# Eight PSUM banks shared out anew in the first layer of a four-layer attention kernel

## The chip, the cores and the metric

One core of one Trainium2 chip (trn2). The metric is the device time of one execution in microseconds; lower is better. All data are float32.

## The reference, cut to what matters

Four layers run one after another on x (16 x 112 x 256) with a context (16 x 375 x 256). The change is in the first layer. For each batch entry it computes, in essence:

```
xn  = layernorm(x) * gamma
q, k, v, ff = split(xn @ w_fused)          # 16 heads of 64, one shared k and v head, 2 x 1024 for the feed-forward
o   = softmax(causal(rope(q) * 64**-0.5 @ rope(k).T)) @ v
y   = x + o @ w_attn_out + (silu(gate) * value) @ w_ff_out
qc  = (layernorm(y) * gamma) @ w_q ;  kc, vc = split((layernorm(context) * gamma_ctx) @ w_kv)
oc  = softmax(qc * 64**-0.5 @ kc.T) @ vc   # 112 queries against 375 keys, 16 heads
z   = y + oc @ w_out + (silu(gate2) * value2) @ w_ff2
```

The first attention is called own, the second cross.

## The kernel before, in words

Every engine runs a program of its own, written out by hand; semaphores alone join them. A layer is one block, and the next layer starts when all engines have ended it. Layer 0 (`layer0`, L551) takes two batch entries at a time, in `TURNS` = 8 turns; seven of them are the body of a loop on each engine, the last stands behind it.

PSUM has eight banks of 128 x 512 float32. `Ring` (L73) shares some of them out to a list of jobs: job k uses bank k modulo the number of banks, and before TensorE writes it, it waits (`Ring.free`, L93) until the job that used that bank last has been read (`emptied`). Layer 0 has three rings, made at L634 and L635:

- the scores ring `S`: 40 items a turn, 8 of the own phase (four heads in one bank) and 32 of the cross phase (one head each);
- the ring `TR` of transposed probabilities, two banks;
- the product ring `P`: everything else, 69 jobs a turn in the order in which TensorE issues them.

The jobs of `P` in the own phase are f0 to f7 (a gate tile and a value tile of the feed-forward, eight matmul instructions, `project` L499), cT00 to cT11 (transposed context, L735, which write at L740), and sO00 to sO13 (outputs of four heads each). In order: f0 f1 cT00 f2 cT01 sO00 f3 cT10 sO01 f4 cT11 sO02 f5 sO03 f6 sO10 f7 sO11 OT00 OT01 sO12 sO13. Then y0 OT10 OT11 y1 ck0 cv0 ck1 yT cv1, cq0 to cq3, cf0 to cf7 (the last two in the cross phase), cO00 to cO13 with cOT00, cOT01 and xT between them, and at the end of the turn k z0 cOT10 cOT11 v0 v1 q0a q0b z1 q1a ... q3b for the coming turn.

`Attention.tensor` (L290) issues, in step s: scores(s), the transposes of item s-2 (`turns`, L306, write at L313), the values of item s-3 (`values`, L316), and then the side work: f(s), and in steps 1 to 4 one cT. ScalarE (`scalar`, L353) does in step s: the tanh of f(s-1) (`gate`, L862, write at L869), the exponentials of item s (L366, L373), the copy pT of item s-2 (L377), and the copy of the cT. VectorE (`vector`, L381) does in step s: the maxima of item s (L392, which reads the score bank and empties it, and L394; in the cross phase L401, and there ScalarE's L373 empties the bank), then hidden(s-1) (`hidden`, L992: L998 and L1000, the last one empties f(s-1)), then in the cross phase the copy pT (L405), and the outputs of item s-3 (L416, L419). The order within an engine is fixed, so what stands behind a waiting instruction waits too.

The other lines named below: L161 is the matmul of every `project`, L301 and L303 the scores, L331 and L335 the values, L721 and L724 the two halves of an output y or z (`outputs`, L716), L732 the transposed outputs OT, read by ScalarE at L873, L893 ScalarE's copy of v, L1004 VectorE's addition that reads y or z, L1025 VectorE's reading of q, L690 GpSimd's addition of q.

```
def earlier(k, depth, count):
    if k >= depth:
        return k - depth, True
    return max(m for m in range(count) if m % depth == k % depth), False
...
self.lagged(phases, [(0, scores), (LAG_T, turns), (LAG_V, values)], between)
...
self.lagged(phases, [(0, maxima), (0, amid), (LAG_T, turned), (LAG_V, outputs)], between, amid)
```

Of the kernel before, what the change touches and what calls it, by code (L numbers as in the profile page):

```python
# [22 lines left out]
class Signal:  # L23
# [3 lines left out]
    def __init__(self, ctx, nc, name, per_turn):  # L27
        self.sem, self.per_turn = ctx.enter_context(nc.semaphore(name)), per_turn

    def prime(self, eng):  # L30
        if self.per_turn:
            eng.sem_inc(self.sem, self.per_turn)
# [132 lines left out]
def wide(ap, axis, n):  # L165

    ap = ap.unsqueeze(axis)
    shape = list(ap.shape)
    shape[axis] = n
    return ap.to_broadcast(shape)  # L170
# [47 lines left out]
class Attention:  # L218
    def __init__(self, ctx, nc, layer, phases, scored, turned, P):
        self.phases, self.P = phases, P  # L220
        self.owner = [(ph, k) for ph in phases for k in range(ph.items)]
# [29 lines left out]
    def pT_free(self, turn, m):  # L251
# [3 lines left out]
        if ph.closes(k):  # L255
            ring = ph.ring or self.P
            s, n = ring.full, ring.index[ph.job(k)]
# [32 lines left out]
    def tensor(self, pe, i, phases, ident, between=None):  # L290
# [25 lines left out]
        def values(ph, k):  # L316
            m = ph.first + k
            j, r = ph.at(k)
            job, P = ph.job(k), ph.ring or self.P
            bank, w = P.bank(job), ph.dh + 1  # L320
            if ph.val_ready:
                for sem, count in counts(i, *ph.val_ready(k)):
                    pe.wait_ge(sem, count)
            if ph.grouped or r % G == 0:
                for sem, count in P.free(i, job, TR.got(m)):
                    pe.wait_ge(sem, count)
# [224 lines left out]
def layer0(nc, c, x_in, context, x_out, w, prefetch):  # L551
# [5 lines left out]
    ctx = ExitStack()  # L557
    with ctx:
# [19 lines left out]
        banks = [ctx.enter_context(nc.psum_tensor(f"l0_bank{b}", [128, 512], F32)) for b in range(8)]  # L578
# [26 lines left out]
        def cross_values_ready(k):  # L605
            return [P.got(f"cv{k // H}")] if k % H == 0 else []

        own = Phase("s", True, H, DH, lambda j, h: qT[:, h // 2, j * T:(j + 1) * T], lambda j, h: kz[:, j, h % 2, :],
                    lambda j, h, t: v[:, j, :], own_ready, bias=lambda r: wide(c.causal[:T, :], 1, G), val_ready=own_values_ready)
        cross = Phase("c", False, H, DH, lambda j, h: qT[:, h // 2, j * T:(j + 1) * T], lambda j, h: ckz[:, j, h % 2, :],  # L610
                      lambda j, h, t: cv[:, j, t, :], cross_ready, val_ready=cross_values_ready)
# [11 lines left out]
        def own_job(s):  # L623
            return [(own.job(s - LAG_V), "dve")] if s >= LAG_V else []
# [4 lines left out]
        jobs = [job for s in range(own.items + LAG_V) for job in own_job(s) + beside_own.get(s, [])] + chain \  # L629
# [1 line left out]
        names = [job for job, _ in jobs]  # L631
        before_x = names[:names.index("xT")]
        after_x = names[names.index("xT") + 1:names.index("k")]
        P = Ring(ctx, nc, "l0_product", banks[4:8], jobs)  # L634
        A = Attention(ctx, nc, "l0", [own, cross], banks[0:2], banks[2:4], P)  # L635

        x_come, c_come, z_sent = signal("x_come", 16), signal("context_come", 16 * PAIR), signal("z_sent", 16)
        NORMS = ("y", "x", "c")
# [76 lines left out]
        def _(pe):  # L715
# [11 lines left out]
            def output_turned(i, j, half, name, done):  # L727
                for sem, count in P.free(i, name, P.got(done)):
                    pe.wait_ge(sem, count)
                for n in range(4):  # L730
                    t = 4 * half + n
                    last = pe.transpose(P.bank(name)[:, n * T:(n + 1) * T], A.O[:, j, t * 128:(t + 1) * 128], c.ident[:T, :T])  # L732
                last.then_inc(P.full.sem, 1)
# [35 lines left out]
            def own_side(i, s):  # L769
                if s < 8:  # L770
                    project(pe, P, i, f"f{s}", [columns(V["wff"], s), columns(V["wff"], 8 + s)], xT)
                if 1 <= s <= 4:
                    context_turned(i, (s - 1) // KT, (s - 1) % KT)
                if s == 8:
                    for half in range(2):
                        output_turned(i, 0, half, f"OT0{half}", own.job(own.groups - 1))

            def between_phases(i):
                pe.wait_ge(weights.sems["out"], weights.count("out"))
                outputs(i, "y0", 0, V["wao"], V["wfo"], "f7", "OT01")  # L780
                for half in range(2):
                    output_turned(i, 1, half, f"OT1{half}", own.job(own.items - 1))
                outputs(i, "y1", 1, V["wao"], V["wfo"], "f7", "OT11")
                pe.wait_ge(weights.sems["cross"], weights.count("cross"))
                context_keys(i, 0)
                context_values(i, 0)
                context_keys(i, 1)
                turn_tokens(pe, c, P, i, "yT", xhat, normed.this(NORMS.index("y")))
                context_values(i, 1)
                for t in range(HT // 2):  # L790
                    project(pe, P, i, f"cq{t}", [columns(V["wq2"], 2 * t), columns(V["wq2"], 2 * t + 1)], xT, P.got("yT"))
                for f in range(6):
                    gate_and_value(i, f)
# [4 lines left out]
            def cross_side(i, s, coming):  # L798
                if s < 2:
                    gate_and_value(i, 6 + s)  # L800
                elif s in (22, 26):
                    output_turned(i, 0, (s - 22) // 4, f"cOT0{(s - 22) // 4}", cross.job(H - 1))
                elif s == 30:
                    if coming:
                        turn_tokens(pe, c, P, i, "xT", xhat, normed.this(NORMS.index("x")))
                    else:
                        P.pass_over(pe, "pe", i, ["xT"])

            def turn_ending(i, coming):
                if coming:  # L810
                    keys(i)
                else:
                    P.pass_over(pe, "pe", i, ["k"])
                pe.wait_ge(weights.sems["cross_out"], weights.count("cross_out"))
                outputs(i, "z0", 0, V["wo2"], V["wf2"], "cf7", "cOT01")
                for half in range(2):
                    output_turned(i, 1, half, f"cOT1{half}", cross.job(cross.items - 1))
                if coming:
                    values(i)
                    queries(i, 0)  # L820
                else:
                    P.pass_over(pe, "pe", i, ["v0", "v1", "q0a", "q0b"])
                outputs(i, "z1", 1, V["wo2"], V["wf2"], "cf7", "cOT11")
                if coming:
                    for t in (1, 2, 3):
                        queries(i, t)

            def turn(i, coming):
                A.tensor(pe, i, [own], c.ident, lambda s: own_side(i, s))
                between_phases(i)  # L830
                A.tensor(pe, i, [cross], c.ident, lambda s: cross_side(i, s, coming))
                turn_ending(i, coming)

            prime(pe, "pe", [A.S, A.TR], [A.values])
            pe.wait_ge(zeroed, 4)
# [18 lines left out]
        def _(act):  # L854
# [40 lines left out]
            def gate_before(i, s):  # L895
                if 1 <= s <= 8:
                    gate(i, s - 1)

            def own_side(i, s):
                if 1 <= s <= 4:  # L900
                    context_turned(i, (s - 1) // KT, (s - 1) % KT)
                if s == 8:
                    for half in range(2):
                        output_turned(i, 0, half, f"OT0{half}")

            def between_phases(i):
                for half in range(2):
                    output_turned(i, 1, half, f"OT1{half}")
                context_keys(i, 0)
                context_values(i, 0)  # L910
                context_keys(i, 1)
                tokens_turned(i, "yT", c.column["L0_gamma_ca"])
                context_values(i, 1)
                for t in range(HT // 2):
                    name = f"cq{t}"
                    act.wait_ge(P.full.sem, P.count_full(i, name))
                    act.activation(qT[:, 2 * t:2 * t + 2, :].rearrange("p a b -> p (a b)"), P.bank(name)[:, 0:2 * TP],
                                                 ACT.Copy, scale=DH ** -0.5).then_inc(P.emptier(name).sem, 1)
                for f in range(6):
                    gate(i, 8 + f)  # L920
# [12 lines left out]
            def turn_ending(i, coming):  # L933
                for half in range(2):
                    output_turned(i, 1, half, f"cOT1{half}")
                if coming:
                    values(i)
                else:
                    P.pass_over(act, "act", i, ["v0", "v1"])

            def turn(i, coming):
                A.scalar(act, i, [own], lambda s: own_side(i, s), lambda s: gate_before(i, s))
                between_phases(i)
                A.scalar(act, i, [cross], lambda s: cross_side(i, s, coming))
                turn_ending(i, coming)
# [2013 lines left out]
```

## Time and profile before

| | |
|---|---|
| median of 3 runs | 4230.74 us (4230.36 to 4244.27) |
| the profiled execution | 4239.7 us, span 4238.0 us |
| TensorE matmuls (PE) | 3909.1 us busy, 92% of the span |
| VectorE (DVE) / ScalarE (ACT) | 1881.8 us, 44% / 1614.5 us, 38% |
| granted TensorE clock, mean | 0.959 of full speed |
| layer 0 in the trace | 0 to about 1250 us |

All rows are of the one profiled execution. PE is a matmul on TensorE, PEld a weight load that runs beside matmuls, DVE is VectorE, ACT ScalarE, POOL GpSimd. Times are microseconds from the start of the span. The ends of matmuls are modelled, so the start of a weight load is the best mark of when TensorE goes on to a new group. A clock of 1.00 is 2.4 GHz, 0.50 is 1.2 GHz.

### The profile page before, as it was taken

Reading aid. Unit: us, or ns where it says so; the run is one execution under the profiler, and the core shown is the slowest. Engines: PE = TensorE matmul, PEld = TensorE weight load, DVE = VectorE, ACT = ScalarE, POOL = GpSimd, SP = SyncE. Lnnn points to the kernel's source line nnn. Section 1 sums busy time; section 2 is a strip of 40 time slices with the busy share of each in tenths; the row PEclk is TensorE's granted clock in tenths of the full one; section 3 lists DMA queues with packets and bytes.
Section 4 is the critical chain, followed back from the end, with each engine's and each line's share of the span. In section 5 each row is a group of like instructions: output and inputs, shape, how many; then the busy total and the mean of one; then the engine's idle time right before and its main releaser. Section 6 shows DMA issues by size and latency. Waiting matters only on the chain. (4 is left out here: it accounts for less than half of the span.)

```text
span 4238.0 us, 68913 instructions
## 1 busy us (share of the span) xinstructions
PE 3909.1 (92%) x23128; PEld 3193.6 (75%) x23128; DVE 1881.8 (44%) x5419; ACT 1614.5 (38%) x3709; POOL 320.5 (8%) x379
## 2 busy tenths in 40 slices
PE   7999999999978999999996999999999997888888
PEld 6888888888867778888774777777777775666666
DVE  3554544545434544555542323323323323546544
ACT  2232333323323433334332454454454443333333
POOL 1000000000001111001100000000000001111110
PEclk9999999999997999999998999999999998899998
DMA  4000000000002000000002000000000000000000
GB/s 167 4 10 13 10 4 13 11 3 13 3 24 94 13 8 12 12 5 12 10 3 75 7 13 7 7 13 7 7 13 7 7 7 21 11 16 16 15 14 5
DMA packets 64014, 75.10 MB, mean 18 GB/s; under 512 B 8336, under 2 KB 61168, under 8 KB 62704
## 3 DMA queue, kind: packets, MB, share of 16 engines
q1 hardware_dynamic: 63728, 71.42, 5.4%
q8 instruction: 163, 2.67, 0.3%
q14 instruction: 123, 1.01, 0.1%
HBM read 64.01 MB, written 7.40 MB: 17 GB/s over the span
## 5 line engine op out<-in xcount | busy, mean ns | idle before, releaser
L313 PEld LDWEIGHTS l_bank<-identity,l_p 112*125 112x125 f32 (+1 forms) x3456 | 516.6, 178 | 244.3 <-issue 18.5
L335 PE MATMUL l_bank<-l_cv,l_pT 125*112 125x65 f32 (+2 forms) x5376 | 640.7, 253 | 54.4 <-ACT l_pT L377 45.4
L161 PE MATMUL l_bank<-l_xT,weights_of_layers_and 128*128 128x224 f32 x3072 | 665.3, 371 | 27.2 <-ACT l_xT L2643 8.5
L335 PEld LDWEIGHTS l_bank<-l_cv,l_pT 125*112 125x112 f32 x5376 | 601.6, 178 | 69.0 <-ACT l_pT L377 32.3
L161 PEld LDWEIGHTS l_bank<-l_xT,weights_of_layers_and 128*128 128x128 f32 x3072 | 595.5, 199 | 55.3 <-ACT l_xT L2643 10.1
L313 PE MATMUL l_bank<-identity,l_p 112*125 112x112 f32 (+1 forms) x3456 | 545.3, 270 | 8.8 <-ACT l_p L366 7.7
L373 ACT ACTIVATE l_p<-l_bank,l_nm 112x375 f32<-112x375 f32 x512 | 293.3, 573 | 487.1 <-DVE l_nm L401 486.6
L303 PE MATMUL l_bank<-l_ckT,l_qz 128*112 128x375 f32 x1024 | 424.3, 498 | 7.2 <-DVE l_qz L1518 7.2
L370 ACT ACTIVATE l_p<-l_p,l_nm 112x375 f32<-112x375 f32 x384 | 233.2, 607 | 470.6 <-DVE l_nm L398 469.2
L366 ACT ACTIVATE l_p<-l_p,l_nm 112x112 f32<-112x112 f32 x768 | 234.8, 376 | 431.8 <-DVE l_nm L394 431.5
L401 DVE TENSOR_REDUCE l_nm<-l_bank 112x1 f32<-112x375 f32 x512 | 279.8, 546 | 204.6 <-PE l_bank L303 201.3
L377 ACT ACTIVATE l_pT<-l_bank 125x336 f32<-125x336 f32 (+1 forms) x576 | 266.4, 464 | 42.8 <-PE l_bank L313 42.8
L161 PE MATMUL l_bank<-l_cT,weights_of_layers_and 128*128 128x375 f32 x704 | 262.8, 500 | 19.9 <-ACT l_cT L2047 17.8
L398 DVE CUSTOM_DVE_ANT_0 l_p<-l_bank,weights_of_layers_and 112x375 f32<-112x375 f32 x256 | 139.1, 543 | 280.4 <-issue 279.5
L405 DVE COPY l_pT<-l_bank 125x336 f32<-125x336 f32 x512 | 254.7, 497 | 14.7 <-PE l_bank L313 13.2
L161 PE MATMUL l_bank<-weights_of_layers_and,l_cT 128*125 128x512 f32 (+2 forms) x768 | 249.2, 462 | 0.0
L460 POOL TENSOR_TENSOR l_ve<-l_mv,eps 112x2 f32<-112x2 f32 (+1 forms) x89 | 17.3, 195 | 2944.4 <-DVE l_mv L454 2944.4
L303 PE MATMUL l_bank<-l_ckz,l_qT 128*112 128x375 f32 x512 | 211.6, 495 | 0.1
L331 PE MATMUL l_bank<-l_v,l_pT 112*112 112x65 f32 (+1 forms) x1536 | 187.1, 262 | 23.2 <-ACT l_pT L377 21.0
L331 PEld LDWEIGHTS l_bank<-l_v,l_pT 112*112 112x112 f32 x1536 | 179.2, 189 | 33.7 <-issue 32.3
L161 PE MATMUL l_bank<-weights_of_layers_and,l_OT 128*112 128x256 f32 x704 | 174.7, 401 | 26.3 <-ACT l_OT L2654 15.9
L303 PEld LDWEIGHTS l_bank<-l_ckT,l_qz 128*112 128x112 f32 x1024 | 152.1, 177 | 58.0 <-issue 28.9
(244 smaller groups left out, 4859.6 us busy)
## 6 DMA issues: line engine op xcount, KB each, us to landing
l_cx<-in_ctx SPq DMA_DIRECT2D x64, 375.0 KB
x_after_layer<-l_z SPq DMA_DIRECT2D x24, 224.0 KB, 2.4
l_x<-x_after_layer SPq DMA_DIRECT2D x24, 224.0 KB, 2.7
weights_of_layers_and<-in_L_xattn_w_fused SPq DMA_DIRECT2D x1, 2048.0 KB, 9.8
weights_of_layers_and<-in_L_xattn_w_ff SPq DMA_DIRECT2D x1, 2048.0 KB, 12.0
weights_of_layers_and<-in_L_xattn_lin_W SPq DMA_DIRECT2D x2, 1024.0 KB, 11.6
weights_of_layers_and<-in_L_xattn_sa_wkv SPq DMA_DIRECT2D x1, 2048.0 KB, 16.3
weights_of_layers_and<-in_L_xattn_ca_wkv SPq DMA_DIRECT2D x1, 2048.0 KB, 21.2
```

What stands on the lines that cost most here:

```text
L161: last = pe.matmul(out, left, right, start=(k == 0), stop=(k == len(pairs) - 1))
L303: last = pe.matmul(bank[:T, 0:S2], ph.q(j, r), ph.k(j, r), start=True, stop=True)
L313: last = pe.transpose(bank[:ph.keys, g * T:(g + 1) * T], p[:, m % PD, g * ph.keys:(g + 1) * ph.keys], ident[:T, :T])
L331: last = pe.matmul(bank[:T, g * w:(g + 1) * w], pT[:T, m % PD, g * T:(g + 1) * T], ph.val(j, r * G + g, 0), start=True, stop=True)
L335: last = pe.matmul(bank[:T, g * w:(g + 1) * w], pT[:ph.keys, m % PD, t * T:(t + 1) * T], ph.val(j, r, t), start=(t == 0), stop=(t == ph.ti ...
L366: last = act.activation(own, own, ACT.Exp, bias=nm[:, c:c + 1])
L370: act.activation(own, own, ACT.Exp, bias=nm[:, ph.col0 + k:ph.col0 + k + 1], scale=-1.0).then_inc(self.probs.sem, 1)
L373: act.activation(p[:, m % PD, 0:S2], S.bank(m)[:T, 0:S2], ACT.Exp, bias=nm[:, ph.col0 + k:ph.col0 + k + 1]).then_inc(S.emptier(m).sem, 1)
L377: self.turned(act, i, ph, k, lambda out, src: act.activation(out, src, ACT.Copy))
L398: dve.tensor_tensor_reduce(p[:, m % PD, 0:S2], S.bank(m)[:T, 0:S2], ph.bias(r), -1.0, 3.0e38, ALU.add, ALU.min, nm[:, ph.col0 + k:ph.col0 ...
L401: dve.tensor_reduce(nm[:, ph.col0 + k:ph.col0 + k + 1], S.bank(m)[:T, 0:S2], AX.X, ALU.max, negate=True).then_inc(self.neg_max.sem, 1)
L405: self.turned(dve, i, ph, k, lambda out, src: dve.tensor_copy(out, src))
```

## The change

The first layer's banks are shared out anew: scores three banks for two, products three for four; the ring of transposed probabilities keeps two, but other ones. Nothing else differs; the waits follow from the number of banks.

```
-        P = Ring(ctx, nc, "l0_product", banks[4:8], jobs)
-        A = Attention(ctx, nc, "l0", [own, cross], banks[0:2], banks[2:4], P)
+        P = Ring(ctx, nc, "l0_product", banks[5:8], jobs)
+        A = Attention(ctx, nc, "l0", [own, cross], banks[0:3], banks[3:5], P)
```

## Rows read from the trace of the kernel before

**Rows 1.** Busy time by stretch, layer 0: stretch, length, busy per engine, clock, DMA.

```profile
0.00:1250.00 1250.00, 1200.76 (x7706) 1065.30 (x7707) 618.26 (x1545) 393.22 (x933) 66.91 (x96) 1.00 0.07 21
```

**Rows 2.** Waits of PE, 47.7 to 1240 us: total, times, longest.

```profile
PE l_bank L313 <- ACT l_p L366: 4.5, 5, 0.9
...
PE l_bank L301 <- DVE l_p L392: 3.4, 5, 1.0
...
PE l_bank L331 <- ACT l_pT L377: 1.8, 5, 0.4
```

**Rows 3.** Busy time by stretch, steady cross phase of turn 1.

```profile
306.00:316.00 10.00, 10.00 (x72) 8.17 (x71) 6.33 (x15) 4.22 (x8) 0.00 (x0) 1.00 0.01 2
```

**Rows 4.** Timeline, turn 0, step 4: start, duration, engine, line; [idle before <-releaser].

```profile
59.77 0.87 PEld L301 LDWEIGHTS l_bank<-l_kz,l_qT 128*112 128x112 f32 x8
...
60.86 0.62 DVE L392 TENSOR_TENSOR l_p<-l_bank,causal 112x448 f32<-112x448 f32 x1 [1.31 <-PE l_bank L301]
...
61.74 1.44 PEld L161 LDWEIGHTS l_bank<-l_xT,weights_of_layers_and 128*128 128x128 f32 x8
...
62.47 0.39 DVE L1000 SCALAR_TENSOR_TENSOR l_hid<-l_u,l_bank 128x224 f32<-128x224 f32 x1
```

**Rows 5.** Timeline, turn 1, steps 2 and 3.

```profile
203.51 0.62 DVE L392 TENSOR_TENSOR l_p<-l_bank,causal 112x448 f32<-112x448 f32 x1 [5.00 <-issue]
...
204.26 1.03 PE L301 MATMUL l_bank<-l_kz,l_qT 128*112 128x112 f32 x8 [0.97 <-DVE l_p L392]
...
204.82 1.22 ACT L366 ACTIVATE l_p<-l_p,l_nm 112x112 f32<-112x112 f32 x4 [25.78 <-DVE l_nm L394]
...
206.19 0.56 PE L313 MATMUL l_bank<-identity,l_p 112*112 112x112 f32 x4 [0.89 <-ACT l_p L366]
...
206.50 1.44 PEld L161 LDWEIGHTS l_bank<-l_xT,weights_of_layers_and 128*128 128x128 f32 x8
...
206.74 0.39 DVE L1000 SCALAR_TENSOR_TENSOR l_hid<-l_u,l_bank 128x224 f32<-128x224 f32 x1
...
207.93 0.44 PEld L740 LDWEIGHTS l_bank<-identity,l_cx 125*128 125x128 f32 x3
...
208.64 0.39 DVE L1000 SCALAR_TENSOR_TENSOR l_hid<-l_u,l_bank 128x224 f32<-128x224 f32 x1
...
210.15 0.97 PE L331 MATMUL l_bank<-l_v,l_pT 112*112 112x65 f32 x8 [0.37 <-ACT l_pT L377]
```

**Rows 6.** Timeline, turn 0, steps 2 and 3.

```profile
55.51 0.44 PEld L740 LDWEIGHTS l_bank<-identity,l_cx 125*128 125x128 f32 x3
...
55.68 0.39 DVE L1000 SCALAR_TENSOR_TENSOR l_hid<-l_u,l_bank 128x224 f32<-128x224 f32 x1
...
57.93 1.44 PEld L161 LDWEIGHTS l_bank<-l_xT,weights_of_layers_and 128*128 128x128 f32 x8
...
58.61 0.39 DVE L1000 SCALAR_TENSOR_TENSOR l_hid<-l_u,l_bank 128x224 f32<-128x224 f32 x1
```

**Rows 7.** Timeline, ending of turn 1.

```profile
330.26 0.42 DVE L1004 TENSOR_TENSOR l_z<-l_bank,l_y 112x256 f32<-112x256 f32 x1 [5.40 <-PE l_bank L724]
...
330.65 0.98 ACT L873 ACTIVATE l_OT<-l_bank 128x448 f32<-128x448 f32 x2 [11.40 <-PE l_bank L732]
330.74 0.86 PEld L161 LDWEIGHTS l_bank<-weights_of_layers_and,l_xT 128*112 128x112 f32 x8
...
331.52 1.63 PEld L161 LDWEIGHTS l_bank<-l_xT,weights_of_layers_and 128*128 128x128 f32 x9
```

**Rows 8.** Timeline, turn 1, between the phases.

```profile
238.63 0.42 DVE L1004 TENSOR_TENSOR l_y<-l_bank,l_x 112x256 f32<-112x256 f32 x1 [6.31 <-PE l_bank L724]
...
239.10 3.30 PEld L721 LDWEIGHTS l_bank<-weights_of_layers_and,l_hid 128*112 128x112 f32 x16
```

**Rows 9.** Turn 5: timeline around a fall of the clock, and one stretch.

```profile
811.03 1.08 PE L301 MATMUL l_bank<-l_kz,l_qT 128*112 128x112 f32 x8 [1.86 <-POOL l_qT L690]
811.80 2.71 PEld L161 LDWEIGHTS l_bank<-l_xT,weights_of_layers_and 128*128 128x128 f32 x8
...
812.00:813.00 1.00, 1.00 (x4) 0.93 (x4) 0.00 (x0) 0.00 (x0) 0.00 (x0) 0.50 0.02 8
```

## The prediction, made before the change was built or run

> **What bounds the kernel now.** I first read the table of stretches for layer 0, the only code that the change touches [rows 1]: TensorE is busy 1200.76 of 1250 us, at a granted clock of 1.00. So layer 0 is TensorE's own program from end to end, and whatever makes TensorE wait there is added to the time. The layers follow one another behind a barrier, so a microsecond lost in layer 0 is lost at the end.
>
> Next the waits of TensorE in the eight turns of layer 0 [rows 2]. Only a few places wait, and one is a wait for a score bank: L301 for DVE L392, 5 times, 3.4 us in all. The others are for data: the transposes for the exponentials (4.5 us), the values for the copied pT (1.8 us). No wait for a product bank (L161 on a reader) stands among them. The cross phase, with 32 of the 40 score items of a turn, is seen in its steady part: 10.00 us busy of 10.00 [rows 3]. There nothing waits, so a third score bank can gain nothing.
>
> The step that matters is one of the own phase, s = 4 of turn 0 [rows 4]. Read it in order of time: the weight load of scores(4) at 59.77; DVE begins with scores(4) at 60.86 (L392, then L394); TensorE begins f4 at 61.74; DVE ends hidden(3), which empties f3's bank, at 62.47 + 0.39 = 62.86. With four banks f4 waited for sO00 and did not need f3's bank. That is the whole case: f4 begins 1.12 us before the previous f bank is empty.
>
> **The change, part by part.** *Scores, two banks to three.* scores(n) waits for item n-3 instead of n-2. It can only remove the wait at scores(2). In turn 1 [rows 5] DVE starts on scores(0) at 203.51 (behind a gap that the trace calls issue, after the loop's jump), frees the bank at 204.13, scores(2) starts at 204.26; exp(0) runs from 204.82 to 206.04 and the transposes of item 0 start at 206.19, having waited 0.89. The exponential depends on DVE's maxima of item 0, not on scores(2). So scores(2) moves up into the gap, the transposes start at the same 206.19, and the 3.4 us of rows 2 become waiting at L313. I take 0. The bounds are 0 and a gain of 3.4 us.
>
> The Trainium skill (Perfetto Trace Analysis, Matmuls) says that independent matmul groups should rotate through different PSUM banks so that emptying one overlaps the next group. For the scores it would have the 3.4 us saved, and the sum below would be 3.4 lower; for the products it speaks against this change. The rows bear it out only for the products.
>
> *Products, four banks to three.* Job k waits for job k-3. Counting along the job list of layer 0 (f0 f1 cT00 f2 cT01 sO00 f3 cT10 sO01 f4 cT11 sO02 f5 sO03 f6 sO10 f7 ...), the new waits are f2 on f0, cT01 on f1, f3 on f2, f4 on f3, f5 on f4, f6 on sO02, f7 on sO03. A wait on a bank ends about 0.13 us after the reader's record: 204.13 to 204.26 [rows 5].
>
> - f4: 62.86 + 0.13 = 62.99 against 61.74 [rows 4]: 1.25 us. It cannot be caught up, as the chain scores(n), maxima(n), hidden(n-1), f(n) closes on itself: scores(n) stands behind f(n-1) in TensorE's program and hidden(n-1) behind maxima(n) in DVE's. From the weight load of scores to f was 61.74 - 59.77 = 1.97 and becomes 62.99 - 59.77 = 3.22. f5 is the same step once more: 1.25.
> - cT01 in turn 0: hidden(1) ends at 55.68 + 0.39 = 56.07, so 56.20 against 55.51 [rows 6]: 0.69. f2 needs hidden(0), done long before.
> - f3 in turn 0: hidden(2) ends at 59.00, moves with scores(3) to 59.69, so 59.82 against 57.93 [rows 6]: 1.89 in all, 1.20 of it new.
> - Sum of turn 0: 0.69 + 1.20 + 1.25 + 1.25 = 4.39.
> - In the turns behind the loop's jump (five like turn 1), f2 meets hidden(0), which ends 206.74 + 0.39 = 207.13: 207.26 against 206.50 = 0.76; cT01 meets hidden(1), 209.03 + 0.13 = 209.16 against 207.93 = 1.23 in all [rows 5]. Of this some 0.4 to 0.5 is taken back, since the values of item 0 waited 0.37 anyway (the weight load a little longer). Then f3 adds 1.25, f4 and f5 1.25 each: 4.5. I use 4.4 for all eight turns.
> - From f6 on, the bank wanted is one that DVE empties a step earlier: no wait. While TensorE stands, ACT and DVE stand too, as they wait for scores. What is late next is scores(n+1) and through it everything; no later wait of the turn absorbs it, since those in the cross phase follow from TensorE's own order.
>
> So 8 x 4.4 = 35.2 us. *The ending of a turn* [rows 7]: v0 now waits for z0, emptied at 330.68: 330.81 against 330.74, 0.07. v1 waits for cOT10 (first of two copies, 330.65 + 0.49 = 331.14) against 330.74 + 0.07 + 0.39: 0.07. q0a waits for cOT11 (331.63 + 0.13 = 331.76) against 331.52 + 0.14: 0.10. Together 0.24, in 7 turns 1.7. *Between the phases* [rows 8]: y1 waits for y0's addition, 239.05 + 0.13 = 239.18 against 239.10: 0.08, in 8 turns 0.6. Every other job of the chain and of the cross phase finds job k-3 read at least one product earlier; what hides these is a product of TensorE's between them, and without it each would cost about the 0.4 us of a reader. The number of instructions, DMAs and bytes is the same, and SP, POOL and ACT issue what they did.
>
> *The clock.* In one turn TensorE stood for 1.86 us in one piece ahead of scores(0); a microsecond later the granted clock was 0.50 (1.2 GHz), and the eight weight loads of an f took 2.71 us [rows 9] instead of 1.44, so 1.27 more. In turn 1 the waits of 0.97 and 0.89 had scores(2) between them, and the clock stayed. With scores(2) moved ahead, those two waits become one of about 2 us in five turns, followed by the wait at f2. From below this costs 0, from above 5 x 1.27 = 6.4, or more if a part of the turn is hit twice. Nearest is the row of 1.86 us, but other work of the stretch (the wait at cT01) covers some of it: I take 2.5.
>
> **Sum:** 35.2 + 1.7 + 0.6 + 2.5 = 40.0 us. Made against the profiled execution's 4239.7 us (span 4238.0) this gives 4279.7; the median of the three runs, 4230.74, is 9.0 lower, and the forecast for the median is 4270.7, say 4271, or 0.95% more. No change could be told from this within some 0.5%, 21 us.
>
> **Rivals.** *A, not slower.* One mechanism: DVE reads f(n-1) early enough, so that no product waits. For it: no wait for a product bank shows today, and DVE is busy only about half of the time [rows 1]. Against it: in rows 4 hidden(3) stands behind maxima(4) in DVE's program and ends 1.12 us late. It decides from the point where hidden(n-1) ends by 61.6 in step 4. Then only the score bank counts: between 4227.3 (3.4 gained) and 4231. If even the waits of 4.5 and 1.8 fell, 4221. Chance 0.03.
>
> *B, a part only.* The stalls come at f4 and f5, but what is lost at cT01 and f3 is taken back in slack that the records don't show (the starts on TensorE are modelled): 8 x 2.5 = 20, less the 3.4: 4247 to 4251. For it: the later stall is the clearest, and turn 1 already shows such a giving back. Chance 0.07.
>
> *C, the clock follows the stalls.* Stalls of 1.25 us in three successive steps lower the clock there too. Each f then costs 1.27 more, three of them in eight turns 30 us on top: 4301. For it: rows 9. Against it: the two waits of 1.86 us together in turn 1, with only scores(2) between them, did not lower it in five turns out of five, and the new stalls stand farther apart. Chance 0.06.
>
> *D, the scores gain and the products lose as forecast.* 4267. It lies within the forecast.
>
> **Chances.** The forecast, D within it, 0.84; A 0.03; B 0.07; C 0.06. The range 4252 to 4285: below, the sum with f3 to f5 alone at 1.25, 1.25 and 0.4 (8 x 2.9 = 23) and nothing for the clock; above, 4.9 a turn (nothing taken back) with 6.4 for the clock, 2.3 for the ending and the spread of the three runs. C and most of B lie outside. Faster by over 0.5% would need 21 us gained where all removable waits are 9.7 us: 0.01. Within 0.5% is A and B: 0.09. Slower 0.90.
>
> **What would show it.** In the changed profile TensorE's waits should list L161 on DVE's L1000 (f3, f4, f5 in each of eight turns, 1.0 to 1.25 us each) and L740 on L1000 (8 times), some 33 us together; L301 on L392 gone, and L313 on L366 grown to about 2 us a time; the step of s = 4 (from one weight load of scores to the next) some 1.25 us longer; the cross phase's 10.00 of 10.00 kept; ACT and DVE busy as before; a digit below 1.00 in the clock near the starts of some turns. Wrong would be: no wait of L161 on L1000 (then A), waits of it at f4 and f5 only (B), or f groups of 2.7 us and more in steps 3 to 5 (C).

## The result, and the profile after

The changed kernel takes 4276.85 us in the median (4260.65 to 4282.59, 6 runs), the kernel before 4242.98 us beside it (4230.36 to 4244.80, 6 runs). The ratio is 1.0072, with a 95% interval of 1.0055 to 1.0090: slower by 0.72%, some 30.5 us of 4243; the two medians lie 33.9 us apart. The forecast was 40.0 us, or 0.95%. The profiled execution took 4266.35 us.

From the page of the changed kernel (span, and TensorE's share of it):

```profile
span 4264.6 us, 68681 instructions
...
PE 3909.9 (92%) x23128; PEld 3187.7 (75%) x23128; DVE 1882.2 (44%) x5419; ACT 1615.3 (38%) x3709; POOL 319.7 (7%) x379
```

The spans differ by 4264.6 - 4238.0 = 26.6 us. To see where, I take a mark that both programs have: the first group of transposes of layer 1, as the grouped lines with their first and last times give it. First the kernel before, then the changed one:

```profile
L1298 PE MATMUL l_bank<-identity,context_turned_or_hidden x4: 421/421/448, 1276.3 to 1276.9; 128*128 128x128 f32 x4
```

```profile
L1298 PE MATMUL l_bank<-identity,context_turned_or_hidden x4: 421/421/447, 1308.1 to 1308.7; 128*128 128x128 f32 x4
```

Counted from the first scores (47.9 and 47.5 us), layer 0 takes 1228.4 us before and 1260.6 us after: 32.2 us more. (Ahead of the mark TensorE stands once, for 22.6 to 23.9 us, between the two layers: 23.9 before, 23.5 after. The measure has that stand in it.) What follows the mark, whose code is the same in both, takes 2961.7 and 2956.5 us, 5.2 us less. That second number is no effect. Over all the executions profiled below, the same unchanged stretch takes between 2947.5 and 2975.4 us. So **layer 0 by itself is the finer measure**, and the experiments are read by it: by the time from the first scores to this mark, beside the ratio of the medians.

Now the waits of TensorE in layer 0 (47.7 to 1275 us) in the changed kernel: total, times, longest, to be held against [rows 2].

```profile
PE l_bank L161 <- DVE l_hid L1000: 25.3, 29, 1.0
PE l_bank L301 <- POOL l_qT L690: 10.6, 5, 2.4
...
PE l_bank L301 <- issue: 1.8, 1, 1.8
...
PE l_bank L313 <- ACT l_p L366: 0.9, 3, 0.3
PE l_bank L740 <- DVE l_hid L1000: 0.7, 3, 0.3
```

The first line is new and is the price of the change: an f product (L161) waits for the DVE instruction that empties the bank of the f before (L1000). L301 on L392, the wait for a score bank, is gone. The second line and the `issue` line, six waits of up to 2.4 us at scores(0) of the turns behind the loop's jump, are also longer than before. I had not foreseen that, and it comes back below.

The step s = 4 of turn 0 in the changed kernel, against [rows 4]: start, duration, engine, line, and in brackets the idle time with what ended it.

```profile
60.83 0.87 PEld L301 LDWEIGHTS l_bank<-l_kz,l_qT 128*112 128x112 f32 x8
...
61.92 0.62 DVE L392 TENSOR_TENSOR l_p<-l_bank,causal 112x448 f32<-112x448 f32 x1 [2.43 <-PE l_bank L301]
...
63.53 0.39 DVE L1000 SCALAR_TENSOR_TENSOR l_hid<-l_u,l_bank 128x224 f32<-128x224 f32 x1
63.97 1.43 PEld L161 LDWEIGHTS l_bank<-l_xT,weights_of_layers_and 128*128 128x128 f32 x8 [1.09 <-DVE l_hid L1000]
...
65.81 0.87 PEld L301 LDWEIGHTS l_bank<-l_kz,l_qT 128*112 128x112 f32 x8
```

The loop of the prediction can be read here. The scores go first, DVE takes their maxima (61.92) ahead of hidden(3) (63.53 to 63.92), and only then does the weight load of f4 start (63.97). From scores to f it is 63.97 - 60.83 = 3.14 us where it was 1.97. The next scores start at 65.81, so the step takes 4.98 us. The kernel before had its next scores at 63.58, a step of 63.58 - 59.77 = 3.81 us:

```profile
63.58 0.87 PEld L301 LDWEIGHTS l_bank<-l_kz,l_qT 128*112 128x112 f32 x8
```

In the steady cross phase nothing has changed against [rows 3]:

```profile
313.00:323.00 10.00, 10.00 (x75) 8.34 (x74) 6.71 (x16) 4.34 (x8) 0.00 (x0) 1.00 0.01 2
```

### The profile page after: what moved, and what is told of

The parts are those of the page before. It is cut to its first block and busy times, and to the rows that moved or that the text cites. A ratio compares the mean times of both kernels' runs of the same rounds, so it can differ in the third digit from the quotient of the medians.

```text
span 4264.6 us, 68681 instructions
## 1 busy us (share of the span) xinstructions
PE 3909.9 (92%) x23128; PEld 3187.7 (75%) x23128; DVE 1882.2 (44%) x5419; ACT 1615.3 (38%) x3709; POOL 319.7 (7%) x379
## 5 line engine op out<-in xcount | busy, mean ns | idle before, releaser
L161 PE MATMUL l_bank<-l_xT,weights_of_layers_and 128*128 128x224 f32 x3072 | 660.7, 369 | 61.8 <-DVE l_hid L1000 25.3
L313 PEld LDWEIGHTS l_bank<-identity,l_p 112*125 112x125 f32 (+1 forms) x3456 | 517.6, 178 | 242.1 <-issue 15.5
L335 PE MATMUL l_bank<-l_cv,l_pT 125*112 125x65 f32 (+2 forms) x5376 | 641.7, 253 | 54.1 <-ACT l_pT L377 44.9
L161 PEld LDWEIGHTS l_bank<-l_xT,weights_of_layers_and 128*128 128x128 f32 x3072 | 591.0, 198 | 93.2 <-DVE l_hid L1000 29.7
L313 PE MATMUL l_bank<-identity,l_p 112*125 112x112 f32 (+1 forms) x3456 | 545.7, 270 | 5.4 <-ACT l_p L366 4.3
L366 ACT ACTIVATE l_p<-l_p,l_nm 112x112 f32<-112x112 f32 x768 | 234.7, 376 | 434.4 <-DVE l_nm L394 434.4
L161 PE MATMUL l_bank<-l_cT,weights_of_layers_and 128*128 128x375 f32 x704 | 262.8, 500 | 19.9 <-ACT l_cT L2047 17.9
L161 PE MATMUL l_bank<-weights_of_layers_and,l_cT 128*125 128x512 f32 (+2 forms) x768 | 249.2, 462 | 0.0
L331 PE MATMUL l_bank<-l_v,l_pT 112*112 112x65 f32 (+1 forms) x1536 | 183.4, 260 | 20.3 <-ACT l_pT L377 18.0
L161 PE MATMUL l_bank<-weights_of_layers_and,l_OT 128*112 128x256 f32 x704 | 176.5, 404 | 27.1 <-ACT l_OT L2654 16.1
## 6 DMA issues: line engine op xcount, KB each, us to landing
weights_of_layers_and<-in_L_xattn_lin_W SPq DMA_DIRECT2D x2, 1024.0 KB, 10.3
```

The source lines that it names most:

```text
L161: last = pe.matmul(out, left, right, start=(k == 0), stop=(k == len(pairs) - 1))
L313: last = pe.transpose(bank[:ph.keys, g * T:(g + 1) * T], p[:, m % PD, g * ph.keys:(g + 1) * ph.keys], ident[:T, :T])
L331: last = pe.matmul(bank[:T, g * w:(g + 1) * w], pT[:T, m % PD, g * T:(g + 1) * T], ph.val(j, r * G + g, 0), start=True, stop=True)
L335: last = pe.matmul(bank[:T, g * w:(g + 1) * w], pT[:ph.keys, m % PD, t * T:(t + 1) * T], ph.val(j, r, t), start=(t == 0), stop=(t == ph.ti ...
L366: last = act.activation(own, own, ACT.Exp, bias=nm[:, c:c + 1])
```

## The experiments

### Which of the two parts costs: the product banks alone

```diff
-        P = Ring(ctx, nc, "l0_product", banks[4:8], jobs)
+        P = Ring(ctx, nc, "l0_product", banks[4:7], jobs)
         A = Attention(ctx, nc, "l0", [own, cross], banks[0:2], banks[2:4], P)
```

> Scores keep two banks, products get three (one bank of the eight is left unused). Theory P (the product banks alone cost, the third score bank is worth nothing): the first matmul of layer 1 (L1298) starts about 32 us later than in the kernel before, within 1.5 us of where the changed kernel has it (1308.1), TensorE waits for L1000 about 25 us in all, L301 again waits for L392 about 3 us. Rival R1 (the third score bank gave some of it back): layer 0 is 3.4 us or more longer than in the changed kernel. Rival R2 (the loss needs the moved score or turned banks): layer 0 as before, 1276.

Measured: 1.0063 (1.0044 to 1.0083), layer 0 in 1259.4 us. TensorE's waits:

```profile
PE l_bank L161 <- DVE l_hid L1000: 25.4, 30, 1.0
PE l_bank L301 <- POOL l_qT L690: 8.3, 4, 2.2
```

The whole loss is there with two score banks: 1259.4 against 1260.6 us with three (whose profile has one fall of the clock in layer 0, this one none). One thing I had expected did not come. The wait of L301 on L392 does not return with two score banks; it appears nowhere in the list. At scores(2) TensorE now arrives late by itself, so the second bank is free in time.

### The changed kernel once more

> The changed kernel once more, on the same chip as the three others, so that their layer 0 and times can be held against it. Theory P: ratio 1.006 to 1.009, L1298 starts 30 to 34 us later than in the kernel before, eight turns each with three waits of 0.95 us at L161 for L1000.

This is the changed kernel without any edit, measured together with the kernels on both sides of this section. Measured: 1.0084 (1.0065 to 1.0102), median 4277.13 us, layer 0 in 1260.5 us. Against the 1260.6 us of the first profile this shows how well layer 0 repeats, while the rest of the span came out at 2975.1 us where it had been 2956.5, in the same program.

### Another order on DVE: hidden(n-1) ahead of maxima(n)

The prediction says that f(n) is late because hidden(n-1) stands behind maxima(n) in DVE's program. These two kernels turn that order round, the first with the banks of the change, the second with those of before:

```diff
-        self.lagged(phases, [(0, maxima), (0, amid), (LAG_T, turned), (LAG_V, outputs)], between, amid)
+        self.lagged(phases, [(0, amid), (0, maxima), (LAG_T, turned), (LAG_V, outputs)], between, amid)
```

> The changed kernel, but in the own phase VectorE does hidden(s-1) ahead of maxima(s) in place of behind it. Theory P (f(n) waits through scores(n), maxima(n), hidden(n-1)): f(s-1)'s bank is empty while scores(s) is still computed, so TensorE's waits on L1000 at f3, f4 and f5 go; layer 0 is some 25 to 30 us shorter than in the changed kernel, L1298 starts at 1276 to 1283. Rival R3 (three banks are too few whatever the order, each f waits for its bank's reader in any case): the waits stay at 1 us each and L1298 at 1305 or later.

> The kernel before (two, two, four banks) with hidden(s-1) ahead of maxima(s) on VectorE in the own phase. Theory P: no product waits there before, so the order is worth nothing in the steady steps; in the five turns where exp(0) is late nothing moves either; L1298 at 1276 within 3 us, ratio 1.000 within its interval. Rival: the maxima, and with them exponentials and transposes, come later by up to 0.8 us a step, and TensorE waits at L313: up to 8 x 2 us slower.

Measured: 1.0150 (1.0130 to 1.0170) with three product banks, layer 0 in 1286.3 us; 1.0143 (1.0121 to 1.0165) with four, 1290.7 us. My expectation was wrong for both: the turned order is far slower than either kernel, by 57.9 and 62.3 us in layer 0. TensorE's waits of the first:

```profile
PE l_bank L331 <- ACT l_pT L377: 20.3, 24, 1.3
...
PE l_bank L740 <- DVE l_hid L1000: 11.6, 8, 2.2
PE l_bank L161 <- DVE l_hid L1000: 9.9, 23, 0.5
```

And of the second, with four banks, the largest wait and one round of its steps:

```profile
PE l_bank L331 <- ACT l_pT L377: 43.0, 33, 3.8
```

```profile
62.12 1.22 ACT L366 ACTIVATE l_p<-l_p,l_nm 112x112 f32<-112x112 f32 x4 [2.06 <-DVE l_nm L394]
...
63.26 0.52 ACT L377 ACTIVATE l_pT<-l_bank 112x448 f32<-112x448 f32 x1
...
64.14 0.34 ACT L869 ACTIVATE l_th<-l_bank 128x224 f32<-128x224 f32 x1
64.51 0.39 DVE L998 SCALAR_TENSOR_TENSOR l_u<-l_th,l_bank 128x224 f32<-128x224 f32 x1 [1.88 <-ACT l_th L869]
64.94 0.39 DVE L1000 SCALAR_TENSOR_TENSOR l_hid<-l_u,l_bank 128x224 f32<-128x224 f32 x1
65.24 0.62 DVE L392 TENSOR_TENSOR l_p<-l_bank,causal 112x448 f32<-112x448 f32 x1
...
66.55 1.22 ACT L366 ACTIVATE l_p<-l_p,l_nm 112x112 f32<-112x112 f32 x4 [2.06 <-DVE l_nm L394]
```

Follow the arrows. DVE's hidden waits 1.88 us for ACT's tanh (L869). The tanh stands in ACT's program behind the exponentials and the copy of pT, and the exponentials wait 2.06 us for the maxima (L394). The maxima now stand behind hidden. That is a ring of two engines which closes once a step, in 66.55 - 62.12 = 4.43 us, where a step of the kernel before took 3.81. I had counted TensorE and DVE and had left ACT out. The ring is not all of the loss. Turn 0, which no jump precedes, is 27.36 us long from scores(0) to scores(7) in both kernels where it was 22.80, and eight times 4.56 is 36 us. The rest lies in the turns behind the jump, and the clock has a part in it: it fell six times in layer 0 with three banks and seven times with four, against once in the kernel before.

The test therefore does not isolate the order on DVE, since it makes a ring of its own. It does show that the maxima are put first for a reason. In the first list f(n) waits less for hidden when hidden comes first, 9.9 us at 23 places instead of 25.3 at 29, but the cT waits more, 11.6 us instead of 0.7. Together that is 21.5 against 26.0 us, so this test neither confirms nor refutes that the order on DVE makes the wait. What speaks for it are the rows of the step s = 4 above.

### Two other ways to divide the eight banks

```diff
         P = Ring(ctx, nc, "l0_product", banks[4:8], jobs)
-        A = Attention(ctx, nc, "l0", [own, cross], banks[0:2], banks[2:4], P)
+        A = Attention(ctx, nc, "l0", [own, cross], banks[0:3], banks[3:4], P)
```

The second has `banks[3:8]` for the products, `banks[0:2]` for the scores and `banks[2:3]` for the turned exponentials.

> Scores three banks, products four as before, and the transposed probabilities one bank in place of two. To be read against the next run, which has the one bank too. Theory P: no wait for L1000 at all; TensorE waits at L313 in every step for the copy of the one transposed bank, and layer 0 is longer by that alone. The third score bank is worth nothing: layer 0 within 1.5 us of the next run; L301 no longer waits for L392. Rival R1: it is 3.4 us or more shorter than the next run.

> Scores two banks, transposed probabilities one, products five. Theory P: as the run before it within 1.5 us in layer 0, since neither the third score bank nor the fifth product bank is ever waited for; L301 waits for L392 about 3 us in all at the heads of the turns, and the waits at L313 for L366 there are 3 us longer in the other. Rival R1: 3.4 us or more longer than that one.

Measured: 1.0033 (1.0017 to 1.0049), layer 0 in 1243.2 us, for 3 + 1 + 4 banks; 1.0031 (1.0011 to 1.0050), 1241.3 us, for 2 + 1 + 5. The waits that matter here, first of 3 + 1 + 4, then of 2 + 1 + 5:

```profile
PE l_bank L313 <- ACT l_p L366: 10.3, 6, 2.0
```

```profile
PE l_bank L313 <- ACT l_p L366: 5.4, 6, 0.9
PE l_bank L301 <- DVE l_p L392: 4.1, 6, 0.9
```

This is a second test of the score bank. With two, TensorE waits 4.1 us for it and then 5.4 us for the exponentials; with three it waits 10.3 us for the exponentials. The two waits have merged into one (9.5 and 10.3), as the prediction said, and the time is the same within 1.9 us, a little more than the 1.5 that I had allowed. The two kernels differ in a fifth product bank as well. It has nothing to remove, since no L161 waits for L1000 with four. Both kernels pay 13 to 15 us against before for the single bank of the turned exponentials.

### The loop taken away

Here the turns of layer 0 are written out one after another, with the banks of before (e7) and of the change (e8):

```diff
-            with pe.Fori(0, TURNS - 1) as i:
+            for i in range(TURNS - 1):
```

and so on ACT and DVE, with the scratch cells of the waits used again in each turn.

> The kernel before with layer 0's seven loop turns written out on TensorE, ScalarE and VectorE (GpSimd and SyncE keep their loops). Theory P: the gap of 4.8 to 5.0 us of VectorE at the head of a turn belongs to the jump back, so it goes, and with it the waits of L301 on L392 (3.4), of L313 on L366 (4.5), of L301 on issue and L690 (3.9) and of L331 on L377 (1.8): layer 0 13 us shorter, L1298 at about 1263. Then the third score bank has nothing at all to remove. Rival: the instructions must be fetched all the same and the gaps stay or are spread: L1298 at 1276 or later.

> The changed kernel (3, 2, 3 banks) with layer 0's loop turns written out on TensorE, ScalarE and VectorE. From the first scores (L301) to the first matmul of layer 1 the kernel before takes 1228.4 us, the changed one 1260.6, the kernel before unrolled 1207.6. Theory P: no head of a turn is late, so every turn is like turn 0, which lost 3.7 us; with the ends of the turns 8 x 3.9 = 31 us over the kernel before unrolled: 1238.6 within 2. Rival: part of the loss belongs to the heads of turns (the jump, the merged wait): under 1230.

Measured: 0.9974 (0.9958 to 0.9989), median 4231.26 us (10 runs, 4220.06 to 4234.84), layer 0 in 1207.6 us for the banks of before; 1.0043 (1.0024 to 1.0062), 1238.3 us for those of the change. The waits of TensorE in layer 0, before's banks first:

```profile
PE l_bank L335 <- DVE l_pT L405: 3.0, 8, 0.4
PE l_bank L161 <- ACT l_xT L859: 1.7, 8, 0.2
PE l_bank L721 <- DVEq L129: 1.1, 1, 1.1
```

```profile
PE l_bank L161 <- DVE l_hid L1000: 22.9, 24, 1.0
...
PE l_bank L740 <- DVE l_hid L1000: 1.4, 8, 0.2
```

Without the jump neither kernel waits at the head of a turn, the clock falls in neither inside layer 0, and the change still costs 1238.3 - 1207.6 = 30.7 us; 1238.3 lies within the 1238.6 +- 2 that I had given. So the loss lies in the steady steps, not in the heads. The counts are the predicted ones to the unit: 24 waits of L161 (f3, f4, f5 in eight turns) and 8 of L740 (cT01 in eight turns). The list has 22.9 + 1.4 = 24.3 us. A recorded wait is shorter than what the step loses, 22.9 / 24 = 0.95 against about 1.15 us (below), and 24 x 0.2 = 4.8 us closes most of the gap to 30.7. The ending of a turn (below) has most of what is left.

The kernel before without its loop is the fastest of all that ran. Layer 0 is 20.8 us shorter, where I had expected 13, and 1.3 us of that lie in TensorE's stand ahead of the mark. In the whole only a part of it arrives: the ratio of 0.9974 is some 11 us, and in e8 too the whole is 18 us slower than the kernel before where layer 0 is only 9.9 us longer. What follows the mark took 2972.7 and 2975.4 us in these two profiles, against 2961.7. So the layers behind run some 8 to 10 us longer when layer 0 is written out; the cause stays open.

### Fewer jobs in the steps of the own phase

The stall needs three jobs in a step: one sO, one f and one cT go through a ring of three banks. Here the four cT jobs leave the steps 1 to 4 and go into the chain between the phases, with the same instructions in all. The first kernel has the banks of the change (e9), the second those of before (e10):

```diff
-        for n, name in enumerate(("cT00", "cT01", "cT10", "cT11")):
-            beside_own[n + 1].append((name, "act"))
...
-        chain = [("y0", "dve"), ("OT10", "act"), ("OT11", "act"), ("y1", "dve"), ("ck0", "act"),
+        chain = [("cT00", "act"), ("cT01", "act"), ("y0", "dve"), ("OT10", "act"), ("OT11", "act"), ("y1", "dve"), ("cT10", "act"), ("cT11", "act"), ("ck0", "act"),
```

> The changed kernel (3, 2, 3 banks) with the four cT jobs taken out of steps 1 to 4 of the own phase and put beside y0 and y1, so that two product jobs are issued a step in place of three, and f(n) waits for sO(n-4) in place of f(n-1). Theory P (the wait comes from three jobs a step in three banks): the 25 us of waits on L1000 go; some 0.2 to 0.5 us a turn are new at y0 and ck0; layer 0 within 5 us of the kernel before, L1298 at 1274 to 1281. Rival R3 (three product banks are too few in any order): L1298 at 1300 or later.

> The kernel before (2, 2, 4 banks) with the four cT jobs beside y0 and y1, the control of the run e9. e9 took 1236.8 us from the first scores to layer 1. Theory P: once the third job of a step is gone, three product banks cost almost nothing against four: this run takes 1232 to 1236 (the fall of the clock in two heads of e9, some 3 us, and its wait at the jump not counted). Rival R3: 1228 or less, so that three banks cost 8 us or more even then.

Measured: 1.0023 (1.0007 to 1.0039), layer 0 in 1236.8 us with three product banks; 1.0010 (0.9998 to 1.0022), 1231.1 us with four. TensorE's waits with three:

```profile
PE l_bank L301 <- POOL l_qT L688: 10.5, 5, 2.2
...
PE l_bank L331 <- ACT l_pT L377: 3.5, 7, 0.8
```

L161 on L1000 is gone entirely, and of the 32.2 us that three banks cost, at most 1236.8 - 1231.1 = 5.7 are left. Of these, two falls of the clock in the profile with three, against none in the one with four, are worth about 2 x 1.3 us. So three product banks are enough where a step has two jobs, and one too few where it has three. The kernel with four banks came out at 1231.1 us, just below the 1232 to 1236 that I had given, and not at the 1228 or less of the rival; the difference from before's 1228.4 is 2.7 us, a little more than the repeats show, and is not resolved.

### The head of the turns

In the changed kernel the wait at scores(0) had grown in six turns: from 0.25, 0.73, 0.32, 0.52, 1.86 and 0.22 us (3.9 together) to 1.85, 2.00, 2.28, 2.35, 1.92 and 2.03 (12.4). Turn 1 of the changed kernel, against [rows 5]:

```profile
195.92 2.84 DVE L981 TENSOR_SCALAR l_cx<-l_cx,l_mv,l_rstd 125x256 f32<-125x256 f32 x6
198.67 0.61 DVE L1025 SCALAR_TENSOR_TENSOR l_qT<-l_bank,l_cos 128x448 f32<-128x448 f32 x1
...
203.24 1.03 PE L301 MATMUL l_bank<-l_kz,l_qT 128*112 128x112 f32 x8 [1.85 <-issue]
...
206.96 0.62 DVE L392 TENSOR_TENSOR l_p<-l_bank,causal 112x448 f32<-112x448 f32 x1 [4.90 <-PE l_bank L301]
```

My reading was this. With three banks, the last query product of a turn, q3b, needs the bank of q2a, whose reader stands in DVE's program behind the 2.84 us of the normalisation (L981). The wait moves to the head, but DVE does not begin the new turn before 4.9 us have passed anyway. So I put the normalisation earlier, ahead of z1, in the changed kernel (e11) and in the kernel before (e12):

```diff
+                if coming:
+                    center(i, "c", context_rows, context_rows)
                 add(i, "z1", 1, z, y)
...
-                    center(i, "c", context_rows, context_rows)
```

> The changed kernel with VectorE's normalisation of the context (L981, 2.8 us) ahead of its addition of z1 in place of behind queries 1, so that q2a is read as soon as it is full. In the changed kernel TensorE stands 1.8 to 2.4 us at scores(0) of six turns (before: 0.2 to 0.7 in five, 1.9 in one). Theory J: q3b now waits for q2a, whose reader is late behind the normalisation; that holds TensorE's sequencer back from its jump, and the fetch behind the jump is no longer covered. Then these waits fall to under 1 us. As VectorE's own gap of 4.8 us sets the head of the turn in any case, the time from first scores to layer 1 stays at 1260.6 less at most 2. Rival J2: the 8.5 us of waits were lost time, and 1252 comes out. Rival J3: the waits have another cause and stay.

> The kernel before with the same move of the normalisation. q3b waits for q1b there, read long before, so theory J expects no change: 1228.4 within 1.5 us from first scores to layer 1, waits at scores(0) of 0.2 to 0.7, and a ratio of 1.000 within its interval.

Measured: 1.0085 (1.0055 to 1.0115), layer 0 in 1260.7 us; and 0.9999 (0.9986 to 1.0012), 1230.2 us. The waits and turn 1 of the changed kernel with the normalisation early:

```profile
PE l_bank L313 <- ACT l_p L366: 9.5, 6, 1.8
...
PE l_bank L301 <- issue: 3.5, 6, 0.7
```

```profile
204.55 1.03 PE L301 MATMUL l_bank<-l_kz,l_qT 128*112 128x112 f32 x8 [0.57 <-issue]
...
209.39 0.62 DVE L392 TENSOR_TENSOR l_p<-l_bank,causal 112x448 f32<-112x448 f32 x1 [4.75 <-issue]
```

The waits at scores(0) fall from 12.4 to 3.5 us, and the time of layer 0 stays at 1260.7 against 1260.6. What was waited at scores(0) is waited at L313 now (0.9 before, 9.5 here). So the longer waits at the head follow from the bank and the normalisation together, and they cost nothing, since DVE's own gap sets when the turn gets going. Of the readings quoted above J2 and J3 fall, and J holds as far as the bank and the time go. Its part on TensorE's sequencer and the fetch behind the jump is not shown by any run. The control came out 1.8 us above before where I had allowed 1.5, and one of its six waits at scores(0) was 1.75 us where I had given at most 0.7; two falls of the clock stand in its profile against one.

## Why the prediction was right, point by point

The case was decided as forecast: slower, by over 0.5%, with the loss at the named products. The predicted 40.0 us stands against some 30.5 us by the ratio, 33.9 between the medians and 32.2 in layer 0. Term by term:

**What bounds the kernel.** Right. The loss stands in TensorE's waits of layer 0, and the cross phase kept its 10.00 of 10.00. The recorded waits of these turns grew from 20.3 to 44.9 us. These 24.6 us are fewer than 32.2, since the step loses more at each of the 24 places than the record of the wait has (0.95 against 1.17 us).

**The third score bank: 0 us.** Right, and twice measured: 1259.4 against 1260.6 us beside three product banks, 1241.3 against 1243.2 beside one turned bank.

The rule of the Trainium skill (Perfetto Trace Analysis, Matmuls), by which groups rotate through different banks, would have had 3.4 us saved as the prediction read it; the runs show no gain. For the products the runs agree with it.

What the prediction said of the form of the wait came true only in part. L301 on L392 vanished, but L313 on L366 shrank from 4.5 to 0.9 us instead of growing to 2 us a time, because TensorE came late to scores(0). With TensorE on time, in e11, the merged waits are there, up to 1.8 us.

**f3, f4, f5: 1.25 us each.** The mechanism was right and the size a little off. The step is 65.81 - 60.83 = 4.98 us. Before, from 59.77 to 63.58 us, it was 3.81, so 1.17 us were added. The term that failed is the 0.13 us from the end of a reader to TensorE's start. It was read at the start of a matmul, a scores group behind L392, and used for the start of a weight load; here hidden(3) ends at 63.92 and the weight load of f4 starts at 63.97, 0.05 us later.

**4.4 us a turn.** In turn 0, from the start of scores(0) to that of scores(7), the changed kernel takes 26.54 us and the kernel before 22.80: 3.74 more, where the steps gave 4.39. Step by step, from one start of scores to the next, the changes are -0.19, 0, +0.48, +1.12, +1.17, +1.17 and 0 us, where I had 0, 0, 0.69, 1.20, 1.25, 1.25 and 0. In turn 1, from DVE's first L392 to the cq0 group, it is 52.40 against 48.46: 3.94 more, and I take that for six turns. (Turns 2, 4 and 6, in which no clock fell, are 4.06 to 4.09 us longer from one first L392 to the next, the 0.16 us of the ending included.) Two at 3.74 and six at 3.94 make 31.1 us where I had 35.2.

The 0.65 us between 4.39 and 3.74 can be read out. Some 0.08 us in each of three steps is the latency above. cT01 cost 0.48 us and not 0.69: the latency has 0.08 of that, and 0.13 is made up by its weight load, which takes 0.31 us behind the wait where it took 0.44. The remaining 0.19 is a wait that the change takes away, and that the prediction did not see. At the start of a turn the rule is not job k-4 or k-3 but the last line of `earlier`: the last job of the turn before whose number leaves the same remainder. A turn has 69 jobs, 0 to 68. So with four banks f0 needs the bank of job 68, q3b, the last product of all, and with three that of job 66, q2b. Before, f0 started just behind DVE's reading of q3b (48.06 + 0.62 = 48.68), 1.07 us after the scores at 47.67:

```profile
48.06 0.62 DVE L1025 SCALAR_TENSOR_TENSOR l_qS<-l_bank,l_sin 128x448 f32<-128x448 f32 x1 [0.82 <-PE l_bank L161]
...
48.74 1.78 PE L161 MATMUL l_bank<-l_xT,weights_of_layers_and 128*128 128x224 f32 x8
```

In the changed kernel f0 starts 0.87 us after the scores at 47.32, ahead of the end of that reading (48.33):

```profile
47.71 0.62 DVE L1025 SCALAR_TENSOR_TENSOR l_qS<-l_bank,l_sin 128x448 f32<-128x448 f32 x1 [0.82 <-PE l_bank L161]
...
48.19 1.44 PEld L161 LDWEIGHTS l_bank<-l_xT,weights_of_layers_and 128*128 128x128 f32 x8
```

Without the loop it is so in all eight turns (1.06 or 1.07 us against 0.87 or 0.88). Behind the jump the late head hides it.

**The ending, 0.24 us.** From the load of L732 to that of q0a, the kernel before took 331.52 - 329.85 = 1.67 us. Now it is 1.83. Before first, then after (two lines):

```profile
329.85 0.93 PEld L732 LDWEIGHTS l_bank<-identity,l_O 112*128 112x128 f32 x8
...
337.24 0.93 PEld L732 LDWEIGHTS l_bank<-identity,l_O 112*128 112x128 f32 x8
...
339.07 2.94 PEld L161 LDWEIGHTS l_bank<-l_xT,weights_of_layers_and 128*128 128x128 f32 x16
```

0.16 us, in seven turns 1.1 instead of 1.7. With the 31.1 this is 32.2 us. That it is layer 0's loss to the tenth is chance: the falls of the clock and the shorter stand ahead of the mark are not in this sum. **y1, 0.08 us:** nothing can be seen of it; the load of y1 starts 0.89 us after that of y0 in both kernels.

**The clock, 2.5 us: wrong.** The granted clock fell in one turn of layer 0 before (turn 5) and in one after (turn 3). In the two kernels with the turned order it fell six and seven times, and in the others in none to two turns. So no more falls came of the change. Two heads of the changed kernel, those of turns 3 and 4:

```profile
517.40 1.83 PE L301 MATMUL l_bank<-l_kz,l_qT 128*112 128x112 f32 x8 [2.28 <-POOL l_qT L690]
...
675.34 1.03 PE L301 MATMUL l_bank<-l_kz,l_qT 128*112 128x112 f32 x8 [2.35 <-POOL l_qT L690]
```

Behind 2.28 us of waiting the group takes 1.83 us, at the lower clock; behind 2.35 us it takes its 1.03. The length of the wait alone does not decide it. (In e2, whose program up to scores(0) of turn 1 differs only in DVE's order, five of six such waits, 1.94 to 2.27 us, were followed by a fall.) Six waits of 1.85 to 2.35 us brought one fall, as the single one of 1.86 us had before. The step that failed is the one from one fall behind one long wait to more falls behind more of them.

**The rivals.** A fell: the waits on L1000 stand there. B, a part only (20 us less 3.4), fell: 30.7 us is lost even where no head takes part, and the 24 waits are f3, f4 and f5 in every turn. Its idea of a giving back was sound for a few tenths of a microsecond a turn: the 0.13 us at cT01 above, and in turn 1, where f2 and cT01 wait 0.49 and 0.47 us, the turn is 3.94 us longer and not the full sum. C fell: the f groups in steps 3 to 5 kept the clock (1.43 us in the row of 63.97). The starts of weight loads, by which all these steps are read, agree from turn to turn within 0.02 us in e7 and e8, so the slack "that the records don't show" on which B leaned was not there.

In sum 40.0 - 32.2 = 7.8 us too much: 4.1 in the turns, 0.6 in the ending, 0.6 at y1, 2.5 in the clock. The median of the changed kernel, 4276.85, is yet above my 4271. The forecast was made from a median of 4230.74 us in three runs, and the kernel before has its median at 4242.98 in six and at 4240 to 4242 in the larger series. So two errors worked against each other: 40.0 us of effect where the medians lie 33.9 apart, some 6 too many, and 12 us too little in the base. That 4271 came so near to 4276.85 is luck in part.

## What to carry to other kernels

Count the jobs that a steady step puts through a ring of buffers: a ring with as many places as a step has jobs ties each product to the reader of the one a step before, and costs at once if that reader stands behind other work in its engine's program. To price such a wait, read in one step how long before the reader's end the next user of the buffer starts, and follow the arrows round until they close, through every engine (leaving out ACT cost me the two kernels with the turned order). A wait for a buffer that is followed by a wait for data within the same few instructions is worth nothing: take it away and the second grows by as much (here 4.1 + 5.4 us became 10.3). And look at the wrap of a ring on its own: there the distance between two users of a buffer depends on the remainder of the number of jobs, and here 69 jobs in four banks tied the first product of a turn to the very last of the turn before.

## What the runs showed of the hardware that I had not expected

- **The jump of a loop costs more than its waits show.** DVE stands for 4.7 to 5.2 us between the last instruction of a turn and the first of the next, in every kernel with the loop (4.90 us above, [rows 5] before). With the turns written out the gap is gone, and layer 0 is 20.8 us shorter, 19.5 of it in the turns: over six jumps, some 3.2 us each. That fetching instructions behind the jump is the cause was only argued; shown is that it goes with the loop.
- **Waits of the same length sometimes lower the clock and sometimes don't.** Of six waits of 1.85 to 2.35 us at the heads of the changed kernel one was followed by a clock of 0.50; in e1 none of six (1.77 to 2.24 us), in e4 one (1.76 to 2.25 us), in e2 five (1.94 to 2.27 us). The kernels without a loop had no fall in layer 0. What decides it is open.
- **The same code varies by 28 us.** Layers 1 to 3, without a changed instruction in them, took 2947.5 to 2975.4 us, while layer 0 repeated within 1.3 us in four kernels that lose the same (1259.4 to 1260.7). The same program alone gave 2956.5 and 2975.1 us. The mean granted clock goes with it: the changed kernel's fastest execution, 4260.65 us, had 0.965 and its slowest, 4282.59 us, had 0.956, and in the 400 us behind the mark the two profiles had 0.93 and 0.89. An effect of less than 0.3% of the whole is better read from the stretch that it touches.
